# Two MoE layers: adding the scaled expert rows in memory, by the scatters, in place of combining them on chip

## The reference, cut to what matters

```python
t = t + _L0_ffn_ref(_ln_t(t), ...)      # then mixing by max pools, then the same with _L1_ffn_ref
# inside an ffn, for every token:
routing = softmax(x @ Wr + br)           # 8 experts
sel_w, sel_idx = top_k(routing, 2)       # layer 0 also divides sel_w by the sum of the two
h = gelu(x @ W1[e] + b1[e])              # 128 -> 512
y = h @ W2[e] + b2[e]                    # 512 -> 128
out = sum over the two chosen experts of share * y
```

## Time and profile before

| | us |
|---|---|
| median of three runs (lowest, highest) | 983.96 (982.83, 988.96) |
| the profiled execution's own time | 989.66 |
| its span | 986.8 |

### The profile page before, as it was taken

One profiled execution on the slowest core, in us unless ns is written; L12 is line 12 of the kernel. 1 busy time (PEld: TensorE's weight loads), 2 busy tenths in 40 slices (PEclk: granted clock), 3 DMA queues, 4 the chain that ended last, 5 costly groups with the idle time before them and its releaser, 6 DMA issues.

```text
span 986.8 us, 14530 instructions
## 1 busy us (share of the span) xinstructions
PE 758.5 (77%) x4233; PEld 656.6 (67%) x4233; DVE 555.5 (56%) x1262; ACT 520.6 (53%) x1407; POOL 608.4 (62%) x597
## 2 busy tenths in 40 slices
PE   0766249999988798975789499976689977988760
PEld 0535238988887586864788387865679866776760
DVE  7967953263500198999867198999985004100005
ACT  1602427475565465653177376653287754555644
POOL 1000057777777777888632777888754777777760
PEclk9886569999999989999589699998699999999985
DMA  9000255455578483544136773543147856656537
GB/s 356 5 0 1 85 204 160 133 176 162 198 238 286 120 308 128 175 149 129 43 106 227 236 257 123 179 150 126 41 119 237 287 193 220 202 160 239 181 101 255
DMA packets 56861, 165.23 MB, mean 167 GB/s; under 512 B 13888, under 2 KB 13901, under 8 KB 56528
## 3 DMA queue, kind: packets, MB, share of 16 engines
q1 hardware_dynamic: 38608, 128.87, 38.5%
q0 software_dynamic: 18176, 35.44, 12.0%
HBM read 134.89 MB, written 31.20 MB: 168 GB/s over the span
## 4 chain that ended last, share of the span: by engine, by line
DVE 32%; PE 31%; POOL 16%; issue 8%; DMA 6%; ACT 5%; SPq 1%; POOLq 0%; DVEq 0%; ACTq 0%
PE h_ps L787 9%; POOL xg L515 8%; PE yT_ps L800 8%; POOL y_rows L524 8%; DVE state L1290 6%; DVE work L1276 5%; DVE work L1271 5%; DVE tok L1240 4%; PE acc_ps L739 4%; DMA xg<-xn_rows,tile_rows 3%; PE turn_ps L722 3%; PE acc_ps L759 3%; DVE work L1284 2%; DMA work<-y_rows 2%; DVE work L986 2%
## 5 line engine op out<-in xcount | busy, mean ns | idle before, releaser
L515 POOL DMA_INDIRECT xg<-xn_rows,tile_rows x284 | 301.5, 1062 | 226.7 <-DVEq L1206 123.8
L524 POOL DMA_INDIRECT y_rows<-yr,tile_rows x284 | 302.4, 1065 | 127.7 <-issue 82.3
L787 PE MATMUL h_ps<-xT,expert 128*128 128x256 f32 (+1 forms) x1376 | 295.3, 365 | 6.8 <-ACT hT L600 5.5
L600 ACT ACTIVATE hT<-h_ps,expert 128x256 f32<-128x256 f32 (+1 forms) x688 | 250.3, 442 | 72.0 <-PE h_ps L787 71.7
L800 PE MATMUL yT_ps<-hT,expert 128*128 128x256 f32 (+1 forms) x1376 | 278.8, 350 | 1.8 <-ACT yT L611 1.8
L787 PEld LDWEIGHTS h_ps<-xT,expert 128*128 128x128 f32 x1376 | 235.3, 205 | 29.3 <-issue 6.6
L800 PEld LDWEIGHTS yT_ps<-hT,expert 128*128 128x128 f32 x1376 | 233.7, 197 | 27.8 <-ACT yT L611 2.2
L1240 DVE SCALAR_TENSOR_TENSOR tok<-work,share,tok 128x128 f32<-128x128 f32 x224 | 62.3, 348 | 293.0 <-DMA work<-y_rows 292.3
L611 ACT ACTIVATE yT<-yT_ps,expert 128x256 f32<-128x256 f32 (+1 forms) x172 | 72.5, 440 | 116.7 <-PE yT_ps L800 116.6
L776 PE MATMUL xT_ps<-ident,xg 128*128 128x128 f32 x284 | 60.2, 294 | 88.4 <-DMA xg<-xn_rows,tile_rows 85.1
L588 ACT ACTIVATE xT<-xT_ps 128x256 f32<-128x256 f32 x144 | 55.6, 386 | 129.1 <-PE xT_ps L776 129.0
(11 more groups left out here) (202 smaller groups left out, 654.3 us busy)
## 6 DMA issues: line engine op xcount, KB each, us to landing
expert<-in_experts SPq DMA_DIRECT2D x172, 514.5 KB, 3.9
work<-y_rows SPq DMA_DIRECT2D x48, 256.0 KB, 6.2
xn_rows<-work SPq DMA_DIRECT2D x16, 512.0 KB, 6.3
xg<-xn_rows,tile_rows POOLq DMA_INDIRECT x284, 3.5
y_rows<-yr,tile_rows POOLq DMA_INDIRECT x284
tok<-in_x_tokens SPq DMA_DIRECT2D x8, 512.0 KB, 7.4
state<-in_x SPq DMA_DIRECT2D x2, 2048.0 KB, 17.4
work<-y_rows SPq DMA_DIRECT2D x8, 512.0 KB, 6.2
```

The lines of the kernel that those rows point to most:

```text
L515: pool.indirect_dma_start(xg[:, s, h, :], None, xn_rows[unit], bass.IndirectOffsetOnAxis(ap=tile_rows[unit % 2][:, 0, at, h:h + 1], axis=0)) \
L524: pool.indirect_dma_start(y_rows[unit], bass.IndirectOffsetOnAxis(ap=tile_rows[unit % 2][:, 1, at, h:h + 1], axis=0), yr[:, s, h, :], None ...
L600: ins = act.activation(hT[:, s, c, cols], h_ps[c // 2][:, c % 2, cols], func, bias=expert[:, t.load(h) % W_RING, BIAS + c:BIAS + c + 1])
L787: mm = pe.matmul(h_ps[c // 2][:, c % 2, cols], expert[:, t.load(h) % W_RING, c * P:(c + 1) * P], xT[:, t.slot(2), cols], start=True, stop= ...
```

## The change

Three things change together.

1. **The rows are added in memory.** Before a unit's tiles begin, SP stores the tokens themselves to memory (`store_base`): for layer 0 to a buffer `sums`, for layer 1 straight to the output. ACT multiplies each expert row by its share while it copies it to `yr`, and the scatter adds the row to its token in memory (`compute_op=ALU.add`). The two lists of outputs, `combine`, the last products and the last stores are gone; between the layers SP loads one list, straight into the tokens.
2. **The share goes along with the slot.** The stored normalised row is 130 numbers long: 128 values, the first expert's share, and the second's share less the first's. A mask of the slots (`second`) says which of the two holds, and ACT forms the slot's share as first + second x difference (two activations of one column per tile).
3. **Order.** [...] The eight two-expert tiles no longer stand at the end of a unit but at tiles 4, 8, 13, 17, 22, 26, 31 and 35, and their first half is scattered ahead of the step's gathers, the second behind them. The steps between the layers stand about three tiles earlier in `WHEN`.

```diff
+SHARES = 2
+SPREAD = [4, 8, 13, 17, 22, 26, 31, TILES - 1]
+SEAT = [FULL + SPREAD.index(j) if j in SPREAD else j - sum(i < j for i in SPREAD) for j in range(TILES)]
+FIRST_LOAD = [j + sum(i < j for i in SPREAD) for j in range(TILES)]
...
-    mixing(0, read=3, state=(6, 7, 8, 9), norm=11, route=(28, 28), slots=30.3, rows=(30, 31, 31.6, 33),
...
+    mixing(0, read=3, state=(5, 6, 7, 7.6), norm=8, route=(25, 25), slots=27.3, base=27, rows=(27, 28, 28.6, 30),
...
-        xn_rows = [nc.dram_tensor(f"xn_rows{u}", [TOKENS, P], F32).ap() for u in range(UNITS)]
-        y_rows = [nc.dram_tensor(f"y_rows{u}", [PAIRS, P], F32).ap() for u in range(UNITS)]
+        xn_rows = [nc.dram_tensor(f"xn_rows{u}", [TOKENS, P + SHARES], F32).ap() for u in range(UNITS)]
+        sums = [nc.dram_tensor(f"sums{b}", [P, BLOCKS, P], F32).ap() for b in range(IMAGES)] + [out[b] for b in range(IMAGES)]
...
+            def store_base(u):
+                sp.wait_ge(s_stats, u + 2)
+                for q in range(QUARTERS):
+                    sp.dma_start(sums[u][:, quarter(q), :], tok[u % IMAGES][:, quarter(q), :]).then_inc(s_base[u], 16)
+
             def store_normalised(u):
+                sp.wait_ge(s_share, u + 1)
                 for q in range(QUARTERS):
                     sp.wait_ge(s_xn, u * QUARTERS + q + 1)
                     sp.dma_start(xn_rows[u].rearrange("(p t) c -> p t c", t=BLOCKS)[:, quarter(q), :],
-                                 work_tok[0][:, quarter(q), :]).then_inc(s_xn_st[u], 16)
...
-                for q in quarters:
-                    for k in range(CHOICES):
-                        sp.dma_start(work_tok[1 + k][:, piece(u, q), :],
-                                     y_rows[u].rearrange("(k p t) c -> k p t c", k=CHOICES, t=BLOCKS)[k][:, piece(u, q), :]) \
-                            .then_inc(s_y_in[u][q], 16)
...
+            def load_outputs(b, *pieces):
+                wait_scattered(b)
+                for g in pieces:
+                    sp.dma_start(tok[b][:, group(g), :], sums[b][:, group(g), :]).then_inc(s_y_in[b][g], 16)
...
                 if t.old(d - RING):
-                    pool.wait_ge(s_xt_ps, t.done(d - RING))
+                    pool.wait_ge(s_xt_sb, t.done(d - RING))
...
-            def scatter(t, d):
+            def scatter(t, d, *halves):
                 s = t.slot(RING, d)
                 unit, at = t.at(d)
-                pool.wait_ge(s_yr_sb, t.done(d))
-                for h in range(t.halves(d)):
-                    pool.indirect_dma_start(y_rows[unit],
-                                            bass.IndirectOffsetOnAxis(ap=tile_rows[unit % 2][:, 1, at, h:h + 1], axis=0),
-                                            yr[:, s, h, :], None, bounds_check=PAIRS - 1, oob_is_err=False) \
-                        .then_inc(s_scat[s], 16)
+                for h in halves:
+                    if h == 0:
+                        pool.wait_ge(s_yr_sb, t.done(d))
+                        if at == 0:
+                            pool.wait_ge(s_base[unit], 16 * QUARTERS)
+                        else:
+                            pool.wait_ge(s_scat[t.slot(RING, d - 1)], t.landed(d - 1))
+                    elif t.parts(d) > 1:
+                        pool.wait_ge(s_scat[s], t.landed(d) - 16)
+                    into = sums[unit].rearrange("p t c -> (p t) c") if unit < IMAGES else out.rearrange("b p t c -> (b p t) c")
+                    pool.indirect_dma_start(into,
+                                            bass.IndirectOffsetOnAxis(ap=tile_rows[unit % 2][:, 1, SEAT[at], h:h + 1], axis=0),
+                                            yr[:, s, h, :], None, bounds_check=TOKENS * (1 + unit // IMAGES) - 1, oob_is_err=False,
+                                            compute_op=ALU.add).then_inc(s_scat[s], 16)
...
+                    due = range(t.halves(-S_BEHIND)) if t.has(-S_BEHIND) and t.at(-S_BEHIND)[1] < TILES - 1 else []
+                    early = 1 if due and t.parts(-S_BEHIND) > 1 else 0
+                    scatter(t, -S_BEHIND, *due[:early])
                     if t.has(G_AHEAD):
                         if t.at(G_AHEAD) == (u + 1, 0):
...
                         begin(u + 1, range(G_FIRST))
-                    if t.has(-S_BEHIND) and t.at(-S_BEHIND)[1] < TILES - 1:
-                        scatter(t, -S_BEHIND)
+                    scatter(t, -S_BEHIND, *due[early:])
                     if t.has(-2) and t.at(-2)[1] == TILES - 1:
-                        scatter(t, -2)
+                        scatter(t, -2, 0)
...
+                unit, at = t.at(d)
+                r = t.slot(RING, d)
+                for h in range(t.halves(d)):
+                    act.activation(share_of[:, r, h:h + 1], xg[:, r, h, P + 1:], ACT.Identity,
+                                   bias=xg[:, r, h, P:P + 1], scale=second[unit % 2][:, SEAT[at], h:h + 1])
                 if t.old(d - 2):
                     act.wait_ge(s_h_ps, t.done(d - 2, 2))
                 act.activation(xT[:, t.slot(2, d), :], xT_ps[:, 0:SLOTS], ACT.Copy).then_inc(s_xt_sb, 1)
...
+                act.wait_ge(s_xt_sb, t.done(d))
                 act.wait_ge(s_yr_ps, t.done(d))
-                act.activation(yr[:, s, :, :], yr_ps[:, 0:HALVES, :], ACT.Copy).then_inc(s_yr_sb, 1)
+                for h in range(t.halves(d)):
+                    ins = act.activation(yr[:, s, h, :], yr_ps[:, h, :], ACT.Copy, scale=share_of[:, s, h:h + 1])
+                ins.then_inc(s_yr_sb, 1)
...
-            def last_products():
-
-                u = UNITS - 1
-                for q in range(PIECES[u]):
-                    act.wait_ge(s_y_in[u][q], 16 * CHOICES)
-                    for t in range(BLOCKS)[piece(u, q)]:
-                        ins = act.activation(work_tok[CHOICES][:, t, :], work_tok[CHOICES][:, t, :], ACT.Copy,
-                                             scale=share[u % IMAGES][:, CHOICES - 1, t:t + 1])
-                    ins.then_inc(s_shared, 1)
...
+                dve.tensor_tensor(z_second, top[:, 1, :], top[:, 0, :], ALU.subtract).then_inc(s_exp_in, 1)
...
+                def shares():
+
+                    dve.wait_ge(s_exp, u + 2)
+                    if layer:
+                        op(dve.tensor_reduce(top[:, 2, :], prob[:, :, 0:EXPERTS], AX.X, ALU.add))
+                    else:
+                        op(dve.tensor_scalar(top[:, 2, :], prob[:, :, EXPERTS], 1.0, None, ALU.add))
+                    if u == 1:
+                        dve.wait_ge(s_xn_st[0], 16 * QUARTERS)
+                    op(dve.reciprocal(share[0], top[:, 2, :]))
+                    dve.scalar_tensor_tensor(share[1], prob[:, :, EXPERTS], -1.0, share[0], ALU.add, ALU.mult).then_inc(s_share, 1)
+
+                if u == 0:
+                    shares()
...
+                if layer and b:
+                    op(dve.tensor_scalar(to[:, 1, :], to[:, 1, :], EMPTY // 2 + TOKENS - 1, TOKENS, ALU.bitwise_and, ALU.bitwise_or))
+                else:
+                    op(dve.tensor_scalar(to[:, 1, :], to[:, 1, :], EMPTY // 2 + TOKENS - 1, None, ALU.bitwise_and))
+                op(dve.tensor_scalar(second[hot][:].rearrange("p j h -> p (j h)"), rows_f[:, 0, :], float(TOKENS + 1), None,
+                                     ALU.is_ge))
                 dve.sem_inc(s_rows, 1)
...
-            def combine(u):
...
-                        for t in range(BLOCKS)[piece(u, q)]:
-                            ins = dve.scalar_tensor_tensor(tok[b][:, t, :], work_tok[1 + k][:, t, :],
-                                                           share[b][:, k, t:t + 1], tok[b][:, t, :], ALU.mult, ALU.add)
...
             def mix(b):
 
-                for t in range(BLOCKS):
-                    ins = dve.bn_stats(stats[:, t, :], tok[b][:, t, :])
+                for g in range(GROUPS):
+                    dve.wait_ge(s_y_in[b][g], 16)
+                    for t in range(BLOCKS)[group(g)]:
+                        ins = dve.bn_stats(stats[:, t, :], tok[b][:, t, :])
                 op(ins)
```

More of the change, by code:

```diff
@@ L69, with mixing @@
 AFTER_UP, AFTER_DOWN = 0.3, 0.6
-def mixing(b, read, state, norm, route, slots, rows, invert):
+def mixing(b, read, state, norm, route, slots, base, rows, invert):
     u = 2 + b
@@ L150, in parts, with seat_runs @@
     def parts(self, d=0):
-        return self.halves(d) if self.at(d)[1] >= FULL else 1
+        return self.halves(d) if self.at(d)[1] in SPREAD else 1
     def load(self, h=0, d=0):
         unit, at = self.at(d)
-        return unit * LOADS + (at if at < FULL else FULL + HALVES * (at - FULL) + h)
+        return unit * LOADS + FIRST_LOAD[at] + h
+def seat_runs():
+    runs = []
+    for j in range(TILES):
+        single = j in SPREAD
+        size = (1 if j == TILES - 1 else HALVES) if single else 1
+        if not single and runs and runs[-1][3] == HALVES:
+            at, n, seat, step = runs[-1]
+            runs[-1] = (at, n + 1, seat, step)
+        else:
```

(11 more changed lines are left out.)

139 lines of the change are left out of this document (50 added, 89 removed).

## The result

The changed kernel takes **1288.7 us** (median, 1287.9 to 1302.6), the kernel before beside it 986.3 (982.8 to 989.0): a ratio of 1.310, 95% interval 1.301 to 1.319. The forecast was 1022 us with a range to 1110; what came is the rival that I had named much slower, and dearer than its own upper bound of 1266.

The account below looks back on a forecast made before the run. POOL's queue was taken to bound the tiles. Start +1.0, units 0 to 3 +21.5, +0.2, +2.1, +34.1, tail -22.0 + 1.1 made +38.0 us: a median of 1022 us, range 958 to 1110.

Parts of the forecast that it names:

- the rival that I had named much slower: On POOL, an adding scatter takes from 1.30 us to issue: 1102 us, 1266 at the upper bound; chance 0.20.
- What each adding scatter costs to issue: On POOL: 1.10 us against 1.00 for a plain scatter, bounds 1.00 and 1.99; 7.1 us per unit of 71 scatters.
- the dear case: The much slower rival: on POOL the adding scatter's issue itself grows, from 1.30 us on; 1102 to 1266 us, chance 0.20.
- What the new waits cost: On POOL, a scatter waits for an earlier one's landing, 3.2 us; each uncovered wait costs 1.8 us.
- The uncovered places: Where a scatter directly follows one it must wait for: eight in units 0 and 2, fifteen in units 1 and 3.
- other tiles: Tiles where 3.96 us pass on POOL before the next tile's scatter, covering a landing of 3.2 us: no wait.
- signs of being wrong: Waits under 40 us, waits at other tiles, issue price outside 1.0 to 1.2 us, or tiles waiting for ACT, not POOL.
- The start: Before the first gather: three more small DVE operations, three for the shares filling a 0.78 us wait for PE; +1 us.
- The tail: After the last scatter: the last image's loads, products, sums and stores go; 22.0 us less, 1.1 given back.
- the faster rival: An adding scatter is as cheap as a plain one, and units 1 and 2 gain from a shorter chain: 962 us, chance 0.20.
- The pauses at the ends of units 1 and 2: POOL's idle time there, 33.9 and 19.4 us, takes up those units' added cost but for 0.2 and 2.1 us.
- ACT's four operations: Two one-column activations of about 0.20 us and two copies of 0.32 us per tile, covered by POOL's 5.17 us: no cost.

Follow-up runs that it names:

- the kernel of four kinds: Changed kernel, scatters into rows of their own, no waits; units 0 to 3: adding 128, adding 64, plain 128, plain 64 rows: 1.59, 1.46, 1.01, 0.92 us each.
- the plain kernel with waits: Changed kernel with the add taken out of each scatter and every wait kept: 1097.7 us, ratio 1.107.
- the square: Four medians: adding scatters with waits and shared rows 1288.7 us, without waits and rows apart 1117.1; plain scatters likewise 1097.7 and 984.7.
- the plain kernel without waits and without the spread: Changed kernel with plain scatters into rows of their own, no waits between them, two-expert tiles at a unit's end again: 979.1 us, ratio 0.992.

## Why the prediction was wrong

**"What each adding scatter costs to issue": the step that failed.** I took 1.10 us because the adding scatter is one instruction with one list, as the plain one is. It is 1.61 in the median, and 1.69 in the mean against 1.065. So 284 of them cost 176.8 us in place of the 28.4 I had put down. The bounds of 1.00 and 1.99 held it. The choice between them was made by likeness, where no row had a price, for a term with 284 copies on the bounding queue: at the middle of the bounds, 1.50, the issue alone is +142 us. The argument against the dear case, that gather and scatter differ by only 16 ns, compared two plain forms and said nothing of the adding one.
The fixed and the per-row part, which no row of the kernel before could separate, stand apart in the kernel of four kinds: half of the rows took 0.09 to 0.13 us away, so what my 1.10 lacked is a price of the form, not of the rows.

**"What the new waits cost": right places, wrong sizes.** The uncovered places came where they were counted (but for tile 33 of unit 1, ahead of which the first gathers of unit 2 stand), and on average 2.76 us stood at each (127.1 / 46) in place of 1.8. The landing that I took, 3.2 us, is what an undisturbed one shows (3.26 in the chain above). Its reason, that an adding scatter reads memory as a gather does, was my assumption: the pages count 122.59 MB read in the changed kernel and in the one with plain scatters and waits alike. What was missing is the 0.82 us from the landing to the next issue; I had let POOL go on at once. With the dearer issue, which covers more, 3.26 - 1.91 + 0.82 makes 2.2 us; the rest, some 0.6, goes with slower landings, as 2.3 stood there with the loads cut. The plain kernel with waits shows the same: 2.11 us of idle time ahead of its last scatter, where its landing of 2.24 less the issue of 0.97 would leave 1.27. The "other tiles", for which I forecast no wait, waited 75.9 us: 3.96 us of cover (4.5 with the dearer issue) is not enough for a landing of up to 8.9 us (that one was issued at 303.30, while SP's four stores of normalised rows ran, 301.18 to 304.70); with the weight loads cut 22.0 were left. I had read 7.3 us as the slowest gather and kept it as a bound for the sum, but never asked how many scatters would meet such a load.

**Put into my own sum,** the measured sizes give 284 x 0.622 + 46 x 2.76 - 53.3 of pauses - 17.4 of tail - 0.3 = +233 us, and with the 75.9 us at the other tiles and 9 us of gathers +318, against +313 measured. These sizes come from the same trace, so this only shows that the sum lacks no large term. The mechanism was the right one; three sizes in it were not: the issue, the wait at an uncovered place, and the wait at the other tiles, put at nothing. Two of the prediction's own signs of being wrong came: the issue price left 1.0 to 1.2, and the other tiles waited too.

**The rest.** The start was right within 1.3 us: the three operations for the shares run from 102.02 to 102.85 and fill the wait for PE, 0.78 us before, and the first gather begins at 128.95. The tail went as forecast, but 17.4 us and not 20.9: the span ends 5.7 us behind the last scatter's end, 7.2 behind its start, where I had expected some 3. DVE begins the statistics of unit 1 at 427.90, 6 us behind the last scatter of unit 0 (421.9), against 24.7 us before, and it wins nothing, as said; by the square it would have won nothing with cheap scatters either, with this table, so the 15 to 31 us that the faster rival counted on in the middle were not there. The pauses at the ends of units 1 and 2 are taken up by the later POOL: the idle time ahead of gathers, without the start and the 0.30 us, is 7 us against 22. ACT's four operations stayed hidden, though a one-column activation took 383 ns in the mean and not some 200: in the plain kernel without waits and without the spread POOL waited 2.6 us longer for the row copies than before.

## What to carry to other kernels

A form of instruction that the trace does not show, on the queue that bounds, times its count, is the term to keep wide: measure it alone before the rest is worked out, here with one kernel of four kinds of scatter. Adding in memory, with the waits that this kernel puts between its scatters, turned independent transfers into a chain here, and each uncovered link cost landing plus wake-up (3.26 and 0.82 us), not issue alone (whether the sums need all of these waits, no run tested: where they were left out, each pair had a row of its own); count the links that no other work of that queue covers, and price the landing with the loads that run beside it. And bound the prize first: a kernel with the dear part simply left out showed that, as the rest stood, under 1% could be won.

## What the runs showed of the hardware

- An adding scatter of 128 rows of 512 B keeps POOL busy for 1.61 us against 1.00. An estimate from the medians with 128 and 64 rows (1.593 and 1.463 us adding, 1.008 and 0.923 plain): 0.5 us of the difference goes with the instruction, and a row takes 2.0 ns against 1.3.
- Each row that it adds stands in the profile as a packet of its own. The page's rows of packets and of the queue (packets, MB) of the plain kernel with waits, then those of the changed kernel:

```profile
DMA packets 51677, 157.26 MB, mean 145 GB/s; under 512 B 13301, under 2 KB 13316, under 8 KB 51344
...
q0 software_dynamic: 18176, 35.73, 12.6%
```
```profile
DMA packets 83485, 157.28 MB, mean 121 GB/s; under 512 B 16520, under 2 KB 49288, under 8 KB 83152
...
q0 software_dynamic: 49984, 35.75, 20.7%
```

  The first is 32 packets for each of 568 transfers; in the second, if the gathers still take 284 x 32, 144 are left for an adding scatter, for the same bytes. Of 512 B to 2 KB there are 15 packets in the first and 32768 in the second, which is 4 x 8192, one for each row added.
- Its landing, counted from the start of the issue, is 2.7 us at best against 2.1 for the plain one, and went up to 8.9 in the changed kernel (6.3 for the plain one in the kernel with waits, 7.6 in the kernel of four kinds).
- From a landing to the issue that waited for it pass some 0.8 us, whichever form it is (0.82 and 0.84 in the chains above); ahead of the scatter at 1286.64, which waited for a landing at 1285.25, it was 1.39.
